# Attention kernel: rows of query maxima by small transfers instead of transpositions

## The reference

```python
# main branch: 16 heads, 128 + 64 query/key dims, through low-rank projections
scores = einsum('bhqd,bhkd->bhqk', qf, kf) * D_Q ** -0.5
probs = softmax(scores, axis=-1)
main_out = einsum('bhqk,bhkd->bhqd', probs, v).reshape(b, s, H * D_V) @ o_w.T
# pattern branch: 16 heads of 16 dims
p_scores = einsum('bhqd,bhkd->bhqk', pq, pk) * PD ** -0.5
p_probs = softmax(p_scores, axis=-1)
pattern_out = einsum('bhqk,bhkd->bhqd', p_probs, pv).reshape(b, s, HID) @ sp_o_w.T
return gates[..., 0:1] * main_out + gates[..., 1:2] * pattern_out
```

## Time and profile before

| | |
|---|---|
| median of 3 runs | 868.13 us (868.11 to 871.94) |
| profiled execution | 870.45 us, of which the span from the first to the last instruction is 868.7 us |
| PE, PEld | busy 802.5 us (92%), 463.8 us (53%) |
| VectorE | busy 590.9 us (68%) |
| GpSimd | busy 430.6 us (50%) |
| ScalarE | busy 398.4 us (46%) |
| mean granted clock of TensorE | 0.972 |

### The profile page before, as it was taken

How to read it: one execution, slowest core, us unless ns; L and a number is a source line. 1 busy time by engine, 2 the same in 40 slices (tenths; PEclk the granted TensorE clock), 3 DMA queues, 4 the chain that set the end, 5 groups by cost and what they waited for, 6 DMA issues and landing times. The chain is left out here.

```text
span 868.7 us, 12785 instructions
## 1 busy us (share of the span) xinstructions
PE 802.5 (92%) x4964; PEld 463.8 (53%) x4964; DVE 590.9 (68%) x680; ACT 398.4 (46%) x499; POOL 430.6 (50%) x255
## 2 busy tenths in 40 slices
PE   5878988999999999999999999999999997999885
PEld 5663554455555554555555545545555553468754
DVE  3745765766677576856785776677666889874646
ACT  3332444555455545554555555555545553520321
POOL 1414209654856574468439552865485543530222
PEclk9979999999999999999999999999999999899978
DMA  9479462007201620351044105300621018101001
GB/s 246 175 203 286 76 169 30 10 14 147 62 1 36 112 62 2 72 114 49 13 98 114 34 13 132 71 19 14 116 62 50 25 51 312 40 14 61 0 1 49
DMA packets 92704, 68.52 MB, mean 79 GB/s; under 512 B 61858, under 2 KB 71396, under 8 KB 92388
## 3 DMA queue, kind: packets, MB, share of 16 engines
q1 hardware_dynamic: 92644, 67.71, 30.2%
HBM read 42.02 MB, written 17.04 MB: 68 GB/s over the span
## 5 line engine op out<-in xcount | busy, mean ns | idle before, releaser
L966 POOL TENSOR_TENSOR acc<-acc,em 128x1024 f32<-128x1024 f32 x96 | 237.2, 2470 | 96.5 <-ACT em L1024 96.4
L1117 DVE TENSOR_REDUCE m2p<-xb 128x2 f32<-128x1024 f32 x128 | 155.2, 1220 | 77.5 <-PE xb L1281 77.1
L1125 DVE TENSOR_REDUCE m<-xb 128x2 f32<-128x1024 f32 x128 | 155.7, 1219 | 63.1 <-PE xb L1281 63.0
L1015 ACT ACTIVATE ep<-xb 128x1024 f32<-128x1024 f32 x128 | 131.1, 1024 | 111.7 <-PE xb L1281 111.7
L1024 ACT ACTIVATE em<-xb 128x1024 f32<-128x1024 f32 x128 | 131.1, 1024 | 102.0 <-PE xb L1281 92.5
L1316 PE MATMUL pvm<-em,cpair 128*64 128x512 f32 x512 | 138.3, 618 | 7.4 <-ACT ctxr L1070 7.4
L929 POOL TENSOR_TENSOR rot<-rot,sin 128x512 f32<-128x512 f32 x32 | 40.9, 1278 | 116.2 <-DMA rot<-raw 116.2
L1281 PEld LDWEIGHTS xb<-pq,pk 49*128 49x128 f32 x256 | 23.9, 184 | 101.0 <-issue 81.3
L966 POOL TENSOR_TENSOR acc<-em 128x1024 f32<-128x1024 f32 x16 | 38.1, 2378 | 64.7 <-PE xb L1424 50.9
L1327 PE MATMUL pvp<-ep,vp 128*32 128x512 f32 x512 | 69.1, 612 | 0.0
L1281 PE MATMUL xb<-pq,pk 49*128 49x512 f32 x256 | 64.3, 499 | 0.0
(11 more groups left out here) (282 smaller groups left out, 1297.3 us busy)
## 6 DMA issues: line engine op xcount, KB each, us to landing
rot<-raw SPq DMA_DIRECT2D x128, 64.0 KB, 2.0
pk<-spqk_d SPq DMA_DIRECT2D x48, 128.0 KB, 4.3
sums<-rec_d SPq DMA_DIRECT2D x32, 128.0 KB, 2.9
ctx_d<-ctxr SPq DMA_DIRECT2D x14, 256.0 KB, 2.0
pq<-spqk_d SPq DMA_DIRECT2D x48, 64.0 KB, 2.3
wraw<-wst_d SPq DMA_DIRECT2D x7, 384.0 KB, 5.8
em<-in_o_w SPq DMA_DIRECT2D x1, 2048.0 KB, 7.8
vp<-vp_d SPq DMA_DIRECT2D x8, 256.0 KB, 4.8
```

The source lines that it names most:

```text
L966: pool.tensor_tensor(acc[:, :, :], before, em[:, j:j + 2, :], ALU.add).then_inc(added, 1)
L1015: act.activation(ep[:, j:j + 2, :], src[:, :, :], ACT.Exp, scale=PAT_SCALE).then_inc(ep_ready, 1)
L1117: dve.tensor_reduce(m2p[:, t, 2 * tp:2 * tp + 2, kt], src[:, :, :], AX, ALU.max).then_inc(x_dve, 1)
L1125: dve.tensor_reduce(m2[:, q, t, :, kt], src[:, :, :], AX, ALU.max).then_inc(x_dve, 1)
```

## The change

The tiles mT and pT, their places in the steps, their transpositions, their copies by ScalarE, `mrp` and the memset of `ms` are gone. VectorE's partial maxima are written in another order, so that the small reductions give, in each partition, **four neighbouring queries per head** (query 4 p + t in partition p, column t). To get this the pm and mm tiles load as weights every fourth query column, starting at t (`pq[:, b, tp, t::4]`, and `queries = slice(q * HALF + t, (q + 1) * HALF, 4)`), instead of 128 adjacent ones. SP carries the result to the row by transfers from 128 partitions of four fp32 each into 512 adjacent fp32 of one partition: four per slot for the pattern heads (`pattern_rows`), two per half for the main heads (`main_rows`). T 0 waits for `mrow_in` as before, M 0 and M 8 for the new `mr_in` instead of ScalarE's copy. VectorE's small reductions wait that the transfers of the slot before have read `ms` or `msp`. In SP's queue `pattern_rows(v)` stands where the old pattern transfers stood, `main_rows(v, 0)` right behind it, and `main_rows(v-1, 1)` behind the store of L884, ahead of the gather of the first half. In slot 0 both thus stand ahead of the stores of `vo`, and in slot 8 `main_rows(7, 1)` stands behind `load_epilogue`.

```diff
@@ order of the tiles @@
-    [("mm", 1), ("pT", 0), ("vo", 0), ("mm", 2)],
+    [("mm", 1), ("vo", 0), ("mm", 2)],
...
-    [("mm", 7), ("vo", 3), ("mm", 8), ("mT", 0)],
+    [("mm", 7), ("vo", 3), ("mm", 8)],
...
-        if v <= NP and s == 7:
-            step.append(("mT", 1))
-        if v < NP and s == 15:
-            step.append(("mT", 0))
...
-        if v < NP and s == 13:
-            step.append(("pT", 0))
@@ SP @@
+            def pattern_rows(v):
+                sp.wait_ge(pm_ready, v + 1)
+                for hh in range(4):
+                    at = 64 * (hh % 2) + 3 * PD
+                    sp.dma_start(pq[at:at + 1, v % 2, hh // 2, :].rearrange("o (p t) -> o p t", t=4).bitcast(F32),
+                                 msp[:, hh, :].bitcast(F32)).then_inc(mrow_in, 16)
+            def main_rows(pair, q):
+                if pair == 0 and q == 0:
+                    sp.wait_ge(zeroed, 1)
+                sp.wait_ge(mm_ready, 2 * pair + q + 1)
+                for h in range(2):
+                    sp.dma_start(mr[64 * h:64 * h + 1, half_of(q)].rearrange("o (p t) -> o p t", t=4).bitcast(F32),
+                                 ms[:, q, h, :].bitcast(F32)).then_inc(mr_in[q], 16)
...
+                if 1 <= v <= NP:
+                    main_rows(v - 1, 1)
...
-                    x_emptied(sp, v, ("pT", 0))
-                    for hh in range(4):
-                        at = 64 * (hh % 2) + 3 * PD
-                        sp.dma_start(pq[at:at + 1, v % 2, hh // 2, :].bitcast(F32),
-                                     mrp[hh:hh + 1, :].bitcast(F32)).then_inc(mrow_in, 16)
+                    pattern_rows(v)
+                    main_rows(v, 0)
@@ VectorE @@
-                    dve.tensor_reduce(m2p[:, t, 2 * tp:2 * tp + 2, kt], src[:, :, :], AX, ALU.max).then_inc(x_dve, 1)
+                    dve.tensor_reduce(m2p[:, 2 * tp:2 * tp + 2, t, kt], src[:, :, :], AX, ALU.max).then_inc(x_dve, 1)
...
-                            x_wait(dve, v - 1, ("pT", 0))
+                            dve.wait_ge(mrow_in, 64 * v)
...
-                    dve.tensor_reduce(m2[:, q, t, :, kt], src[:, :, :], AX, ALU.max).then_inc(x_dve, 1)
+                    dve.tensor_reduce(m2[:, q, :, t, kt], src[:, :, :], AX, ALU.max).then_inc(x_dve, 1)
...
+                        pair = v - q
+                        if pair:
+                            dve.wait_ge(mr_in[q], 32 * pair)
+                        dve.tensor_reduce(ms[:, q, :, :], m2[:, q, :, :, :], AX, ALU.max).then_inc(mm_ready, 1)
@@ PE @@
-                    x_emptied(pe, it + q, ("mT", q))
+                    pe.wait_ge(mr_in[q], 32 * (it + 1))
...
-                    mm = paired(out, [(pq[:, b, tp, t * P:(t + 1) * P], pk[:, b, tp, half_of(kt)])], 3 * PD)
+                    mm = paired(out, [(pq[:, b, tp, t::4], pk[:, b, tp, half_of(kt)])], 3 * PD)
...
-                    at = (4 * q + t) * P
-                    queries, keys = slice(at, at + P), half_of(kt)
+                    queries, keys = slice(q * HALF + t, (q + 1) * HALF, 4), half_of(kt)
```

More of the change, by code:

```diff
@@ L461 @@
     [("pm", 15), ("oT", 8), ("mm", 0), ("oT", 9)],
[1 row of a table removed]
[1 row of a table added]
     [("mm", 3), ("vo", 1), ("mm", 4)],
     [("mm", 5), ("vo", 2), ("mm", 6)],
[1 row of a table removed]
[1 row of a table added]
 ]
-BY_ACT = ("mT", "pT", "S", "oT", "vo", "o", "sv")
+BY_ACT = ("S", "oT", "vo", "o", "sv")
 def unit_at(v, p):
@@ L551, in attention @@
         mr = sb("mr", [P, S], F32R)
-        mrp = sb("mrp", [4, HALF], F32R)
-        m2 = sb("m2", [P, 2, 4, 2, 2])
-        ms = sb("ms", [P, 2, 4, 65])
+        m2 = sb("m2", [P, 2, 2, 4, 2])
+        ms = sb("ms", [P, 2, 2, 4], F32R)
         m2p = sb("m2p", [P, 4, 4, 2])
-        msp = sb("msp", [P, 4, 4])
+        msp = sb("msp", [P, 4, 4], F32R)
         ctxr = sb("ctxr", [P, HALF])
@@ L610, in attention @@
         mrow_in = sem("mrow_in")
+        mr_in = [sem(f"mr_in{i}") for i in range(2)]
         wraw_in = sem("wraw_in")
@@ L917, in _ @@
             pool.memset(ones[:, :], 1.0).then_inc(cleared, 1)
-            pool.memset(ms[:, :, :, :], 0.0).then_inc(zeroed, 1)
             pool.memset(mr[:, :].bitcast(F32), 0.0).then_inc(zeroed, 1)
@@ L1024, in x_tile @@
                     act.activation(em[:, j:j + 2, :], src[:, :, :], ACT.Exp, scale=MAIN_SCALE).then_inc(em_ready, 1)
[L1025 to L1033, removed]
                 elif kind == "oT":
@@ L1124, in x_tile @@
                     q, t, kt = i // 8, i // 2 % 4, i % 2
-                    dve.tensor_reduce(m2[:, q, t, :, kt], src[:, :, :], AX, ALU.max).then_inc(x_dve, 1)
+                    dve.tensor_reduce(m2[:, q, :, t, kt], src[:, :, :], AX, ALU.max).then_inc(x_dve, 1)
                     if i % 8 == 7:
                         x_emptied(dve, v, tile)
-                        if q == 0 and v == 0:
-                            dve.wait_ge(zeroed, 2)
-                        dve.tensor_reduce(ms[:, q, :, 0:65:64], m2[:, q, :, :, :], AX, ALU.max).then_inc(mm_ready, 1)
+                        pair = v - q
+                        if pair:
+                            dve.wait_ge(mr_in[q], 32 * pair)
+                        dve.tensor_reduce(ms[:, q, :, :], m2[:, q, :, :, :], AX, ALU.max).then_inc(mm_ready, 1)
             def main_reciprocal(n):
@@ L1292, in main_scores @@
                 if s % NT == 0:
-                    x_emptied(pe, it + q, ("mT", q))
+                    pe.wait_ge(mr_in[q], 32 * (it + 1))
                 if (it, s) == (0, 0):
                     pe.wait_ge(sel_set, 3)
-                    pe.wait_ge(zeroed, 2)
+                    pe.wait_ge(zeroed, 1)
                 return paired(out, [(xkh, xqh), (xkh, xql), (xkl, xqh), (ykh, yqh), (ykh, yql), (ykl, yqh),
@@ L1409, in x_tile @@
                                            oT[:, hd, :], start=True, stop=True)
[L1410 to L1417, removed]
                 elif kind == "S":
@@ L1429, in _ @@
                     for tile in xs[v][s]:
-                        if tile[0] != "pT" or v == 0:
-                            x_tile(v, tile)
+                        x_tile(v, tile)
                     if s == 0 and v >= 2:
@@ L1439, in _ @@
                         pattern_values(v - 1, (s - 3) // 2)
-                    if ("pT", 0) in xs[v][s] and v:
-                        x_tile(v, ("pT", 0))
 PAIRED = ("kxh", "kxl", "qxh", "qxl", "qyh", "qyl")
```

## The result

The changed kernel takes 863.67 us (median of 12 runs, 862.47 to 867.85) against 869.02 us for the kernel before in the same comparison (12 runs, 867.32 to 872.08): ratio 0.9936, interval 0.992 to 0.9952, or 5.35 us less. The profiled execution took 864.78 us, its span 862.9 us, 5.8 us less than the span of before.

What follows compares the result with a forecast made beforehand. TensorE (PE) alone was taken to fill ordinary slots. Terms -15.2 + 2.3 + 5.5 + 2.0 = -5.4 us gave 862.7 us against the median 868.13; range 856 to 882.

Steps and rivals of the forecast that it cites:

- PE's stream: Slots 1 to 7: removing 7 pT, 14 mT and 7 stalls ahead of mT saves 15.2 us.
- Rows in ordinary slots: M 0 and M 8 of ordinary slots: rows land 2.5 us after the first issue, in time, so no cost.
- Rival D: All slots: small pieces land 5.6 us after the first issue, M 0 and M 8 are late, +16 us, 879; chance 0.08.
- Strided loads: pm and mm weight loads at every fourth column: just hidden beside matmul pairs except after bank waits, 2.0 us lost.
- rival B: 384 pm and mm pairs: strided loads no longer hide, starting at 0.22 us of streaming; above 894 or 928 us; chance 0.24.
- Slot 0 to 1: SP's queue: rows ahead of the vo stores delay slot 1's stacks and first rotation, 2.3 us lost (bounds 0 and 3).
- PE's wait for `pk`: Slot 1: the stacks are issued 2.3 us later, so PE waits longer for `pk`.
- M 0 gets its row before that matters: Slot 0 to 1: M 0's row arrives before the late stacks matter, so no further loss was counted.
- Slot 8: M 8's row lands behind the epilogue loads; PE waits some 13 us, 5.5 us lost (bounds 0 and 7).
- Rival C: Slot 8: the rows aren't held up by the load burst and land by 734; -10.9, 857 us; chance 0.12.

Runs made afterwards that it cites:

- e2: The changed kernel with adjacent query columns as pm and mm weights again instead of every fourth: 861.23 us, ratio to before 0.9911.
- e1: The kernel before with only the strided pm and mm weight loads (every fourth query column): 871.29 us against 868.88, ratio 1.003.
- e9: The changed kernel with pm and mm loads at every third column and all six key loads of M at every eighth: 873.01 us, ratio to before 1.0059.
- e8: The changed kernel with pm and mm loads at every second column and T loads at every eighth: 873.28 us, ratio to before 1.0046.
- e6: The changed kernel with the first three stores of vo ahead of main_rows(0, 0) in slot 0: 859.8 us, ratio to before 0.9904.
- e3: The changed kernel with the context store and the rows for M 8 ahead of the 23 epilogue loads in slot 8: 856.0 us, ratio to before 0.9851.
- e4: The kernel before with the context store ahead of the epilogue loads in slot 8: 864.24 us against 868.88, ratio 0.9948.
- e0: The changed kernel again, unaltered, timed on the same chip as the others: 862.81 us against 868.88 for the kernel before, ratio 0.9929.
- e7: The changed kernel with both SP queue edits, those of e3 (slot 8) and e6 (slot 0): 852.51 us against 868.59, ratio to before 0.9805.
- e11: The kernel of e7 with VectorE's division in slot 8 moved from step 14 to step 12: 847.36 us against 870.64, ratio to before 0.9737.

## Why the prediction was right, and where its terms were off

**PE's stream (-15.2).** 2.17 us per slot were predicted. Without strided loads 2.25 are measured (`e2`), with them 2.08 (82.40 to 80.32). The account by distances between starts was right, the stall included. In the six slots 2 to 7 this is the -12.5 of the table.

**Rows in ordinary slots (0).** From the end of the reduction to M 0's matmul 4.3 us are left (278.63 to 282.95, load 0.2 earlier), to M 8's 5.0; predicted were 4.1 and 4.8 to the load. Two issues and a median landing of 2.0 us fit in this, at 2.5 after the first issue as taken. Rival D is out: PE waits for the row in no slot but 1 and 8.

**Strided loads (+2.0): right, by a thin margin.** 1.6 (`e2`) to 2.4 us (`e1`), and rival B is out. The load itself was put too low: up to 290 ns were expected, 306 to 309 measured, 0.12 us more than an adjacent one. By the prediction's own account that is 0.22 us of streaming (an estimate: its 0.10 and these 0.12), just the 0.22 at which rival B was to start. A pair is 0.23 to 0.24 us after an mm load of 306 ns. How thin the margin was, `e9` shows: strided loads in a row of six make each pair 0.017 us longer, and 0.014 in each pm and mm pair would have eaten the gain. The Trainium skill (Advanced Engine Details and Errata, "SBUF Cachelines") wants at least two hits on each 16-byte line. The measured loads agree with where it puts the edge: 185 ns at distance 1, 193 to 208 at 2 (two fp32 of a line), 249 to 252 at 3, 306 to 309 at 4, and hardly more at 8 (309 in `e8`, 316 to 329 in a row of six). Its penalty is real, and it hides here nearly whole.

**Slot 0 to 1 (+2.3): a part was missing.** In the profiled pair slot 1 is 2.6 us longer, where the prediction's terms give +0.1. Slot 1 took 83.06 to 84.54 us in the kernels with the order of before (mean of four 83.79), 84.34 to 86.54 with the changed order (mean of five 85.56; `e8` and `e9`, with other loads, are left out) and 82.61 to 83.45 with that of `e6` (mean of three 83.13). So the late stacks, and what follows them in SP's queue, cost 85.56 - 83.13, some 2.4 us, which is near the predicted term. Some of this is chance: in two of the five (the changed kernel's first profile and `e3`), and in one of the four with the order of before (`e4`), the granted clock fell once more in slot 1, for 3.4 us. And it isn't PE's wait for `pk` that carries it, as predicted (0 to 0.7 us with the changed order), but a wait for ScalarE's `ep` in front of an mm tile: 1.3 to 1.6 us in these five, with the order of `e6` 0 to 0.3. ScalarE's stream has the copy of the rotated queries (137.59) ahead of that `ep` (138.13), and this copy waited 2.69 us for GpSimd, whose rotation starts when the transfers that SP issues behind the stacks have landed (134.91; before 130.62).

The order of `e6` is still 83.13 - (83.79 - 2.2) = 1.5 us above what the shorter stream gives. Here a step of the prediction failed, "M 0 gets its row before that matters". In an ordinary slot the value products stand between the last reduction and T 0, in slot 0 there are none. M 0 waits 2.4 to 2.6 us for its row in every kernel with the change, where it waited 0.57 for ScalarE's copy, and in each of them the lower clock follows. Before (M 0, the second T tile, the mm tile behind `ep`):

```profile
116.23 0.50 PE L1281 MATMUL xb<-qxh,kxh 64*128 64x512 f32 x2 [0.57 <-ACT mr L1028]
...
121.01 0.50 PE L1281 MATMUL xb<-pq,pk 49*128 49x512 f32 x2
...
134.90 0.49 PE L1281 MATMUL xb<-kxh,qxh 64*128 64x512 f32 x2 [1.70 <-ACT ep L1015]
```

After (the last two of them):

```profile
125.16 0.50 PE L1282 MATMUL xb<-pq,pk 49*128 49x512 f32 x2
...
139.19 0.63 PE L1282 MATMUL xb<-kxh,qxh 64*128 64x512 f32 x2 [1.62 <-ACT ep L1024]
```

And in `e6_vo_first` (the last):

```profile
135.72 0.63 PE L1284 MATMUL xb<-kxh,qxh 64*128 64x512 f32 x2 [0.21 <-ACT ep L1026]
```

From T 0 to M 0 it takes 3.06 us instead of 1.06, and from M 0 to the second T tile 6.3 instead of 4.8: 2.0 us for the wait and 1.5 for the lower clock, 3.5 in all. With the order of `e6` some 2 us of them are won back, since waits that PE had before (0.39 for `pk`, 1.70 for `ep`) shrink to 0.2; the 1.5 us are left. In the changed kernel the late queue keeps these waits up, and the whole is about 4 us instead of 2.3.

**Slot 8 (+5.5): right in mechanism, 1.2 too large.** The wait of 12.95 us (13 predicted), the landing 7.2 us after the issue (7 to 8), the restart 46.0 us after the slot's T 0 instead of 46.6 (0.45 predicted, 0.66 found): all as worked out. The work behind the restart, to T 15, grew from 21.7 to 26.7 us, 4.9 instead of 5.9, mostly because the lower clock lasted only to 734.0, 3.8 us after the restart, where the prediction took the 5.4 of before (1.6 us at half speed are 0.8, an estimate). Together +4.3, in `e0` +3.4. Rival C is out: the 23 loads landed one after the other in the order of issue, the last at 729.0, the rows at 729.3 and 730.1. The Trainium skill (DMA: Bandwidth & Descriptors, "Two DMAs through the same engine are not ordered") says that descriptors of one queue start in order, but that this gives no order of completion. Both agree: no row overtook a load, while the first row (729.3) landed ahead of the larger store issued before it (729.7).

**The sum.** -5.4 predicted, -5.35 measured: that close is luck. Two errors, some 1.5 us missed in slot 1 and 1.2 too much in slot 8, cancel. The table's +0.6 ahead of slot 1 and -0.8 behind T 15 are not settled: the first stretch varied from 113.2 to 117.9 us between profiled executions, and from 113.6 to 116.8 between kernels that are alike there.

**What was not asked.** The prediction took the change as given. `e3` and `e6` show that SP's order costs the changed kernel about 9 us (6.8 and 2.2; `e7`: 10.8). Not all of it came with the new rows: 4.6 us of slot 8's part were there before (`e4`). With the store ahead of the loads in both kernels the change is worth 0.9948 - 0.9851, 8.4 us, instead of 5.35. `e11` shows that the gain from the right place is hidden in part by one division's place on VectorE.

## What to carry to other kernels

When a step moves from a compute engine to DMA, its cost is its place in the queue: look at every stage where the usual cover is missing (first slot, last slot) and put the small transfer, and whatever else the engines wait for, ahead of bulk loads. When a hole is closed and less comes out than its length, read the next wait: here a division one engine further on stood behind work that nobody was waiting for. A strided weight load is nearly free in the shadow of a long matmul, and only there; count how many stand in a row and how many start after a wait.

## What the runs showed of the hardware

- A load of 128 fp32 columns takes 185 ns with adjacent columns, 306 to 309 at every fourth and 309 to 329 at every eighth (`e1`, `e8`, `e9`). Beside pairs of 512-column matmuls (0.23 us) each of six such loads in a row costs 0.017 us (`e9`); one with nothing to hide behind costs 0.12 us (`e8`).
- Two transfers from 128 partitions of 16 bytes into one partition: issue 0.47 to 0.60 us each, landing 2.0 us after it, 2.9 us from the end of the reduction to the matmul's load; behind 23 loads of 256 KB and more, with the DMA engines 92% busy, 7.2 us to the landing.
- A PE wait of only 2.4 us in slot 1 was followed by 3.4 us at the lower clock (matmuls of 0.69 instead of 0.39 us), and so it was in every profile of a kernel with the change. A wait of 1.62 us in the same slot (139.19) was followed by 3.4 us more of it from 140.1, one of 1.70 us at the same tile before the change (134.90) by none. In slot 8, 3.8 us at the lower clock followed the wait of 12.95 us.
